# Two-layer decoder, folded wide cross attention: the order of the sum of half tile h+1 and the maximum of h+2 on VectorE, and the place of a batch's turning back on TensorE

## The reference

```
q = einsum('bqm,mhd->bqhd', x, Wq) + bq            # 4 x 512 x 16 x 64
k = einsum('bkm,mhd->bkhd', ctx, Wk) + bk          # 4 x 77 x 16 x 64
v = einsum('bkm,mhd->bkhd', ctx, Wv) + bv
attn = softmax(einsum('bqhd,bkhd->bhqk', q / 8, k))
out = einsum('bqhd,hdm->bqm', einsum('bhqk,bkhd->bqhd', attn, v), Wo) + bo
x = layernorm(x + out)
```

## Time and profile before

| | |
|---|---|
| median of 3 runs | 2390.18 us (2387.64 to 2396.96) |
| the profiled execution, its time | 2394.99 us |
| its span, first to last instruction | 2393.2 us |
| mean granted TensorE clock | 0.866 |
| PE busy | 1842.1 us (77%) |
| PE weight loads busy | 1041.4 us (44%) |
| DVE busy | 1385.4 us (58%) |
| ACT busy | 1035.7 us (43%) |
| POOL busy | 155.9 us (7%) |
| stage e | from 1919.85 us to 2175.10 us of the span |

### The profile page before, as it was taken

The page is one execution under the profiler, slowest core; times in us unless marked ns, Lnnn a source line. Parts: engine busy times, 40 slices in busy tenths (PEclk is TensorE's granted clock), DMA queues, the critical chain, the costliest instruction groups (busy, mean ns, idle before and its releaser), DMA issues. The chain is left out here.

```text
span 2393.2 us, 33578 instructions
## 1 busy us (share of the span) xinstructions
PE 1842.1 (77%) x9665; PEld 1041.4 (44%) x9718; DVE 1385.4 (58%) x4754; ACT 1035.7 (43%) x1970; POOL 155.9 (7%) x281
## 2 busy tenths in 40 slices
PE   3277773873365867799949999999999677777997
PEld 2144442541022323577724444544444345455665
DVE  7398866656365754433358777777677433333445
ACT  3288861651054645334316556566556221111221
POOL 2000003001000000000020000000000021110000
PEclk7699995896588989899969999999999865766999
DMA  2543102402513110100010000000000100000000
GB/s 56 79 46 36 18 3 42 58 11 47 78 13 39 21 21 3 36 19 18 10 36 1 1 1 1 1 1 0 1 1 1 36 2 1 1 0 14 21 20 24
DMA packets 57636, 48.74 MB, mean 20 GB/s; under 512 B 12691, under 2 KB 53047, under 8 KB 57527
## 3 DMA queue, kind: packets, MB, share of 16 engines
q1 hardware_dynamic: 57527, 47.45, 12.5%
HBM read 38.30 MB, written 8.91 MB: 20 GB/s over the span
## 5 line engine op out<-in xcount | busy, mean ns | idle before, releaser
L1432 PE MATMUL ps_s<-d_KZ,d_Q 128*128 128x512 f32 x512 | 265.4, 601 | 16.1 <-issue 6.8
L1580 ACT ACTIVATE d_PR<-d_PR,d_NM 128x512 f32<-128x512 f32 x256 | 184.6, 721 | 189.8 <-DVE d_NM L1511 189.3
L557 DVE TENSOR_REDUCE c_NM<-ps_t 128x1 f32<-128x512 f32 x256 | 169.9, 688 | 99.2 <-PE ps_t L437 97.5
L1507 DVE CUSTOM_DVE_ANT_0 d_PR<-ps_s,d_BH 128x512 f32<-128x512 f32 x256 | 176.2, 688 | 61.6 <-PE ps_t L1440 44.7
L437 PE MATMUL ps_t<-KX,QX 96*128 (+1 forms) x256 | 107.6, 425 | 108.7 <-DVE c_IB L575 47.9
L1440 PEld LDWEIGHTS ps_t<-ident,d_PR 128*128 128x128 f32 x1024 | 121.4, 141 | 150.7 <-issue 132.5
L619 ACT ACTIVATE c_PT<-ps_s 128x1024 f32<-128x1024 f32 x128 | 130.4, 1024 | 128.6 <-PE ps_s L460 126.7
L2282 DVE SCALAR_TENSOR_TENSOR X<-ps_t,GATE,X 128x128 f32<-128x128 f32 x272 | 76.7, 344 | 184.2 <-PE ps_t L2207 184.2
L1587 ACT ACTIVATE d_PT<-ps_t 128x512 f32<-128x512 f32 x256 | 149.9, 586 | 50.7 <-PE ps_t L1440 49.0
L1440 PE MATMUL ps_t<-ident,d_PR 128*128 128x128 f32 x1024 | 156.4, 275 | 10.1 <-ACT d_PT L1587 8.1
L762 ACT ACTIVATE a_PR<-a_PR,a_NM 128x128 f32<-128x128 f32 (+3 forms) x256 | 129.8, 555 | 77.9 <-DVE a_NM L743 77.9
(11 more groups left out here) (330 smaller groups left out, 3237.6 us busy)
## 6 DMA issues: line engine op xcount, KB each, us to landing
QX<-split_parts SPq DMA_DIRECT2D x108, 128.0 KB
KX<-split_parts SPq DMA_DIRECT2D x72, 128.0 KB
f_W<-in_L_ffn_w SPq DMA_DIRECT2D x16, 256.0 KB, 3.1
split_parts<-a_PARTS SPq DMA_DIRECT2D x8, 384.0 KB, 10.0
split_parts<-c_PARTS SPq DMA_DIRECT2D x8, 384.0 KB, 11.2
g_W<-in_L_ffn_w SPq DMA_DIRECT2D x24, 128.0 KB, 2.2
split_parts<-b_PARTS SPq DMA_DIRECT2D x4, 384.0 KB, 10.7
X<-in_x SPq DMA_DIRECT2D x4, 256.0 KB
```

The costliest lines, as they stand in the source:

```text
L557: nc.vector.tensor_reduce(NM[:, qt, j:j + 1], c.ps_t[:, i % 2, :], AX.X, ALU.max, negate=True).then_inc(maxed, 1)
L1432: nc.tensor.matmul(c.ps_s[:, qt % 2, :], Q[:, p % 2, qt * P:(qt + 1) * P], KZ[:, p % 2, i % 2, :], start=True, stop=True).then_inc(scores, 1)
L1507: nc.vector.tensor_tensor_reduce(out=PR[:, h % 2, qt, :], in0=c.ps_s[:, qt % 2, :], in1=BH[:, h, S - P - qt * P:2 * S - P - qt * P], scale ...
L1580: nc.scalar.activation(PR[:, h % 2, qt, :], PR[:, h % 2, qt, :], ACT.Exp, bias=NM[:, h % 2, qt:qt + 1], accum_out=DEN[:, h % 2, qt:qt + 1] ...
```

## The change

On DVE, total(h+1) now stands ahead of lessen(h+2) instead of behind it. On PE and ACT the turning back of a batch moves from h % 8 == 6 to h % 8 == 7. There PE issues back(b), score(h+2), the wait for s_xt, turn(h), weigh(h), where it used to issue back(b), the wait for s_xt, turn(h), score(h+2), weigh(h); the wait for `taken` of h ahead of back(b) goes. LEAD = 2 gives the old distance of the scores a name. No instruction that computes is added or removed.

```diff
--- before.py
+++ after.py
@@ -1791,6 +1791,7 @@
     HH = H // 2
     W = CHUNKS * P
     RING = 3
+    LEAD = 2
     norms = 1 if pre is None else 2
     with ExitStack() as own:
         ONES = c.sb(f"{tag}_ONES", [NPART, P], BF16, own)
@@ -1897,6 +1898,10 @@
                                               start=(half == 0 and i == 0), stop=(half == 1 and i == CHUNKS - 1))
                     mm.then_inc(weighed, 1)
 
+                def ahead(h):
+                    if h + LEAD < HALVES:
+                        score(h + LEAD)
+
                 def back(b):
                     pe.wait_ge(s_n, QT * (b + 1))
                     for i in range(QT):
@@ -1906,16 +1911,17 @@
 
                 pe.wait_ge(s_ones, 1)
                 pe.wait_ge(s_pad, 1)
-                score(0)
-                score(1)
+                for h in range(LEAD):
+                    score(h)
                 for h in range(HALVES):
-                    if h % (2 * QT) == 6 and h > 6:
-                        pe.wait_ge(taken, h)
+                    due = h % (2 * QT) == 7 and h > 7
+                    if due:
                         back(h // (2 * QT) - 1)
+                        ahead(h)
                         pe.wait_ge(s_xt, h // (2 * QT))
                     turn(h)
-                    if h + 2 < HALVES:
-                        score(h + 2)
+                    if not due:
+                        ahead(h)
                     weigh(h)
                 back(B - 1)
 
@@ -1944,7 +1950,7 @@
                 exp(0)
                 exp(1)
                 for h in range(HALVES):
-                    if h % (2 * QT) == 6 and h > 6:
+                    if h % (2 * QT) == 7 and h > 7:
                         columns(h // (2 * QT) - 1)
                     take(h)
                     if h + 2 < HALVES:
@@ -2015,10 +2021,10 @@
                 lessen(1)
                 total(0)
                 for h in range(HALVES):
+                    if h + 1 < HALVES:
+                        total(h + 1)
                     if h + 2 < HALVES:
                         lessen(h + 2)
-                    if h + 1 < HALVES:
-                        total(h + 1)
                     if h % 2 == 0 and h >= 2:
                         add(h // 2 - 1)
                     if h > 3 and h % (2 * QT) in (2, 3, 4, 5)[:1 + norms] and h >= 2 * QT:
```

## The result

The changed kernel takes 2280.43 us (median of 4 runs, 2278.21 to 2285.52) against 2393.18 for the kernel before in 4 runs: ratio 0.9534, 95% interval 0.9506 to 0.9561. The profiled execution has a span of 2276.5 us, 116.7 under that of before.

A forecast was written before the change was run, and what follows sets the result against it. Stage e was taken as bound by a loop of waits closing each half tile. Gains of 107.9 (29 periods) and 5.7 (tail), less 4.4, gave 109: 2390.18 - 109 = 2281 us; own range 2266 to 2300, wider 2264 to 2308.

The forecast's parts named there:

- The loop and its length: Stage e: softmax of 4.86 us from score to turn, the loop closing over two half tiles, 3.66 us each at 2.4 GHz.
- PE's work at 1.2 GHz: Stage e, per half tile: turn 0.91, score 3.44 and weigh 2.21, together 6.56 us.
- The clock: Stage e: after one period of 6.56 us the clock rises to 2.4 GHz and stays, then 28 x 3.66 = 102.5 us.
- the 4.4 us that I took off: Taken off the gain for one stretch of 10 us in which the clock is at 1.2 GHz all the same.
- The batch steps: DVE's statistics and POOL's deviation make PE's turn late by 1.05 us per batch, 3.2 for three; the applying costs nothing more.
- The turning back: Moved step: PE pauses 1.0 us ahead of weigh, plus four transpositions of 0.4; 1.4 each, 2.8 between turn(0) and turn(29).
- The tail: Stage e from turn(29): 16.8 us in place of 22.50, gain 5.7.
- Contention: POOL's multiplication beside DVE's maximum and subtraction: taken as zero; bound of 4.27 us a period, 17 us in 28.
- The sum: turn(0) to turn(29) 115.0 us against 222.9, gain 107.9; with the tail's 5.7, 113.6; less 4.4, gain 109.
- The lower end of the range: 2266 us: below the forecast by 13 if the loops give the bare 3.59 and nothing falls back.

The follow-up runs named there:

- pool runs: One more POOL multiplication per half tile, result unused: on the changed kernel 2295.45 us, ratio 0.9597; on the kernel before 2441.1 us, ratio 1.0242.
- after_copy: The changed kernel run once more, unaltered, beside other kernels: 2273.53 us, ratio 0.9563 to the kernel before.
- order_alone: The kernel before with only the two DVE steps exchanged, the turning back left at h % 8 == 6: 2276.66 us, ratio 0.9526.
- filler_old: The kernel before, old DVE order, with four unused 384-column products on PE after each weigh(h): 2355.98 us, ratio 0.9860.
- move_alone: The changed kernel with DVE's old order, so only the turning back of a batch is moved: 2380.47 us, ratio 0.9969 to the kernel before.
- pool3_new: The changed kernel with three more unused POOL multiplications in each half tile: 2356.14 us, ratio 0.9870 to the kernel before.
- pool1_new: The changed kernel with one more unused POOL multiplication in each half tile: 2295.45 us, ratio 0.9597 to the kernel before.

## Why the prediction was right

Forecast 2281, measured 2280.4. Point by point:

*The loop and its length.* Forecast: 4.86 us from a score's end to turn of the same half tile, and 3.66 a period. Measured: 4.80 from the maximum, with the 0.05 ahead of it 4.85; periods of 3.56 and 3.74, mean 3.65. The pool runs show that it is a loop over two half tiles: an added 1.17 costs 0.6 a period in the new order and 1.17 in the old.

*PE's work at 1.2 GHz* was 6.43 a half tile and not 6.56 (turn(0) to turn(1) in the profile after): I had taken weigh by its duration of 2.21, and the next turn starts 2.09 behind its start. It carried little weight.

*The clock.* Forecast: it rises within the first half tile and stays, less one stretch of 10 us. It rose some 9 us after turn(0), where I had 6.6 (in the second profiled execution, after_copy, some 6.5), and then stayed: the first three periods are 6.43, 4.87 and 3.79, 1.2 over my 6.56 + 2 x 3.66. No fall followed, so most of the 4.4 us that I took off was not needed. Two readings behind this term were loose. The window of the earlier trace rows reaches 0.6 us past the fall, which stands near 2109.7, 1.6 us into a pause; and the longest pause of PE that the trace shows in narrow attention's window is 0.78, not as long as the holes of 1.0 that I set beside it. The traces now have such holes: the three pauses of 1.45 in order_alone left the clock at 1.00. filler_old shows that PE's activity and not the order as such raises it. The terms can be read from the runs: the clock alone takes the 29 periods from 222.9 to 191.2; the open loop without the clock would leave 29 x 6.43 = 186.5 (worked out from one period, not run); both give 115.1. Each alone gives 32 to 36, together 108, because at 2.4 GHz the old loop of 6.43 holds PE back, and at 1.2 GHz PE's own 6.43 does.

*The batch steps.* Forecast: POOL's deviation delays turn by 1.05 at h = 12, 20, 28, and the applying costs nothing more. The timeline at h = 28:

```profile
2033.57 0.86 DVE L1992 BATCH_NORM_STATS2 e_ST<-X 128x6 f32<-128x128 f32 x4
...
2034.46 0.38 DVE L1995 BATCH_NORM_AGGREGATE e_MV<-e_ST 128x2 f32<-128x6 f32 x4
2034.76 0.76 DVE L1978 TENSOR_REDUCE e_DEN<-e_PR 128x8 f32<-128x616 f32 x1
...
2035.24 1.04 POOL L1850 TENSOR_TENSOR e_RS<-e_RS,neghalf 128x4 f32<-128x4 f32 x1
...
2036.25 1.22 POOL L1854 TENSOR_TENSOR e_PR<-e_PR,e_RDEN 128x616 f32<-128x616 f32 x1
...
2037.52 0.53 PEld L1887 LDWEIGHTS ps_t<-ident,e_PR 128*128 128x128 f32 x5 [1.05 <-POOL e_PR L1854]
```

The pause is 1.05, and the next period 3.51: nothing more. That period itself is 4.64, which is 1.0 over the mean. At h = 20 the pause is 1.06, and at h = 12 it is 0.88.

*The turning back.* Forecast 1.4 each: a pause of 1.0 ahead of weigh and four transpositions. At h = 15 the timeline shows the pause at 1.03, and turn(14) to turn(16) takes 5.85 + 2.68 = 8.53 against 7.3, so 1.2:

```profile
1987.89 0.53 PEld L1887 LDWEIGHTS ps_t<-ident,e_PR 128*128 128x128 f32 x5
...
1988.70 0.70 ACT L1938 ACTIVATE e_PT<-ps_t 128x640 f32<-128x640 f32 x1 [1.28 <-PE ps_t L1887]
1989.45 1.19 PEld L1897 LDWEIGHTS ps_f<-e_U,e_PT 128*128 128x128 f32 x10 [1.03 <-ACT e_PT L1938]
```

What I had not seen is that the same step opens the old loop for one half tile in each batch (move_alone). It does not bear on the sum, which has the new order.

*The tail.* Forecast 16.8, measured 17.33 (2041.03 to 2058.36), against 22.5 before.

*Contention.* Forecast none. The groups of stage e in the profile after keep L1971 and L1854 at their old means of 800 and 1217 ns, though they now overlap: the multiplication at 1954.39 covers a maximum and the first 0.3 us of the subtraction at 1955.26:

```profile
L1854 POOL TENSOR_TENSOR e_PR<-e_PR,e_RDEN 128x616 f32<-128x616 f32 x32 | 38.9, 1216 | 75.5 <-DVE e_RDEN L1982 75.5
L1971 DVE TENSOR_TENSOR e_PR<-ps_s,e_M 128x616 f32<-128x616 f32 x32 | 25.6, 800 | 1.1
```

By the Trainium skill ("SBUF — State Buffer", section "Who interferes with whom") an instruction on DVE with a single SBUF input, outside the two-port modes, does not contend with GpSimd; the subtraction is one, and the trace agrees with its 800 ns.

The instruction that the prediction names as hit, the applying, got faster instead. In the kernel before, its mean was 501 ns and its longest 1251, beside a multiplication on POOL of 1217; in the changed kernel it no longer falls under one as a whole, its mean is 346 and its longest 379.

*The sum* was 115.0 for the 29 periods, measured 115.08, and 113.6 for the stage, measured 113.0. The forecast of 2281 took 4.4 less gain, and met 2280.4 because the kernel before, timed again beside the changed one, had a median 3 us higher than in the runs shown at first. The lower end of the range does not come out of its own reason: the bare 3.59 gives 28 x 0.07 = 2.0, and without the 4.4 that is 6.4 under the forecast, not 13. The measured time lies above it by either. That the sums are this near is in part luck: a second profiled execution of the same kernel had 113.8 and a stage of 140.2, and the kernel before had medians from 2382 to 2393 in the sets of runs beside which the others were timed.

## What to carry to other kernels

When an engine's list holds a step that is ready behind one that waits for the bound engine, the loop closes one item earlier than it must; exchanging the two costs nothing and doubles the distance. Draw the loop with its starts from one period of the timeline, and say over how many items it closes: a cost added to a loop over two is paid by half. Where TensorE pauses in such a loop, price its work at both levels of the clock, since an opened loop can bring the higher level with it, and the two gains together were about three times either of them here (one of the two an estimate).

## What the runs showed of the hardware

More work on TensorE made the kernel faster: 128 added products of 384 columns took 33 us off (filler_old), all by the clock. And the busy share of PE alone does not tell the clock: in pool3_new PE was busy 145.12 of 181.27 us (80%) with a mean clock of 0.78, while narrow attention, also at 80%, had 1.00.

The two differ in the length of their pauses. Narrow attention's longest there is 0.78, and pool3_new has many of 2 us and more. Between them lie pool1_new, with 1.00 over 72 us of pauses of 1.3 and a fall only behind its two of 2.2, and order_alone, with 1.00 through pauses of 1.45. No run varied the pause alone, so that its length is what decides is not shown.
